# Two loads moved in the SyncE queue of a fused cross-attention kernel: the first keys ahead of the Wv, Wo and row loads, the first batch's values directly behind their write

## The reference

```python
qh = split_heads(q @ Wq.T + bq); kh = split_heads(k @ Wk.T + bk); vh = split_heads(v @ Wv.T + bv)
scores = einsum('bhqd,bhkd->bhqk', qh, kh) / sqrt(32)
scores = where(mask == 0, -1e9, scores)
e = exp(scores - max(scores)) * mask
probs = e / (sum(e) + 1e-09)
attn = einsum('bhqk,bhkd->bhqd', probs, vh)
x = attn @ Wo.T + bo + q
return (x - mean(x)) / sqrt(var(x) + 1e-05) * ln_g + ln_b
```

## Time and profile before

| | us |
|---|---|
| median of 3 runs (lowest, highest) | 617.98 (617.49, 618.96) |
| the profiled execution, its own time | 615.88 |
| span of its trace | 614.1 |
| busy PE / PEld | 564.5 / 456.9 |
| busy DVE / ACT / POOL | 525.6 / 504.6 / 437.5 |

### The profile page before, as it was taken

The page is one execution under the profiler, slowest core; times in us unless marked ns, Lnnn a source line. Parts: engine busy times, 40 slices in busy tenths (PEclk is TensorE's granted clock), DMA queues, the critical chain, the costliest instruction groups (busy, mean ns, idle before and its releaser), DMA issues.

```text
span 614.1 us, 15264 instructions
## 1 busy us (share of the span) xinstructions
PE 564.5 (92%) x5460; PEld 456.9 (74%) x5460; DVE 525.6 (86%) x801; ACT 504.6 (82%) x2288; POOL 437.5 (71%) x399
## 2 busy tenths in 40 slices
PE   2699398999999999999999999999999999999795
PEld 2588376777878788777877788777878788776574
DVE  4577558789998979898998989898998899899877
ACT  4449669899898989998898989998898999889521
POOL 2704443867588795789778886689678967786787
PEclk9989789999999999999999999999999999999899
DMA  8922730120045310640324412340424312202132
GB/s 310 318 88 57 225 88 1 52 99 3 11 140 188 138 53 10 216 147 3 94 93 155 155 64 75 122 148 3 126 76 141 153 51 104 105 2 99 76 138 102
DMA packets 36198, 64.91 MB, mean 106 GB/s; under 512 B 12443, under 2 KB 14491, under 8 KB 34075
## 3 DMA queue, kind: packets, MB, share of 16 engines
q1 hardware_dynamic: 35979, 63.94, 30.6%
q10 hardware_dynamic: 144, 0.00, 0.0%
HBM read 44.15 MB, written 19.46 MB: 104 GB/s over the span
## 4 chain that ended last, share of the span: by engine, by line
PE 84%; DVE 6%; SPq 5%; DMA 3%; issue 2%; POOL 0%; ACT 0%; DVEq 0%
PE qo_bank L420 54%; PE s_bank L420 17%; PE av_bank L508 11%; DVE E L803 2%; DMA Kd<-TP 2%; PE av_bank L420 1%; DMA Vp<-V_scratch 1%; DVE TP L832 1%; SPq L251 1%; SPq L330 1%; SPq L256 1%; DVE qo_bank L849 1%; DVE bn L855 1%; SPq L304 0%; DVE AT_lo L841 0%
## 5 line engine op out<-in xcount | busy, mean ns | idle before, releaser
L625 ACT ACTIVATE E<-E,neg_max 128x77 f32<-128x77 f32 x1024 | 352.2, 352 | 19.7 <-DVE neg_max L811 19.6
L625 ACT ACTIVATION_READ_ACCUMULATOR E<-E,neg_max 128x1 f32 x1024 | 196.8, 192 | 0.0
L1125 POOL TENSOR_TENSOR E<-E,inv_sum 128x1232 f32<-128x1232 f32 x64 | 145.7, 2279 | 66.6 <-DVE inv_sum L818 66.6
L803 DVE TENSOR_TENSOR E<-s_bank,mask_bias 128x616 f32<-128x616 f32 x128 | 101.3, 791 | 40.7 <-PE s_bank L420 38.9
L420 PE MATMUL s_bank<-Kd,QT_hi 128*128 128x308 f32 x512 | 111.7, 305 | 0.0
L832 DVE STREAM_TRANSPOSE TP<-E 128x1280 f32<-128x1280 f32 x64 | 96.1, 1502 | 4.1 <-PE av_bank L508 3.6
L811 DVE TENSOR_REDUCE neg_max<-E 128x8 f32<-128x624 f32 x128 | 98.5, 781 | 0.4
L420 PE MATMUL s_bank<-Kd,QT_lo 128*128 128x308 f32 x256 | 81.3, 317 | 15.5 <-DVE E L803 11.7
L420 PEld LDWEIGHTS s_bank<-Kd,QT_hi 128*128 128x128 f32 x512 | 84.4, 188 | 4.2
L1143 POOL TENSOR_TENSOR Y<-Y,b_row 128x512 f32<-128x512 f32 x62 | 79.2, 1297 | 4.5 <-ACT Y L642 4.2
L1105 POOL TENSOR_TENSOR xT_lo<-xT_raw,xT_hi 128x1024 fp32r<-128x1024 f32 x30 | 71.7, 2410 | 14.0 <-ACT xT_hi L602 14.0
(11 more groups left out here) (60 smaller groups left out, 790.9 us busy)
## 6 DMA issues: line engine op xcount, KB each, us to landing
Y<-in_x SPq DMA_DIRECT2D x16, 1024.0 KB, 6.1
out_y<-Y SPq DMA_DIRECT2D x64, 256.0 KB, 2.0
xT_raw<-in_xT SPq DMA_DIRECT2D x15, 1024.0 KB, 4.9
Vp<-V_scratch SPq DMA_DIRECT2D x32, 96.0 KB, 2.4
K_scratch<-TP SPq DMA_DIRECT2D x1, 1232.0 KB, 6.8
Y<-in_WqT SPq DMA_DIRECT2D x4, 256.0 KB, 8.4
xT_raw<-in_xT SPq DMA_DIRECT2D x2, 512.0 KB, 6.9
TP<-in_WvT SPq DMA_DIRECT2D x4, 256.0 KB, 7.9
```

Of the source, the lines that this page charges most:

```text
L625: last = cp(e, e, ACT.Exp, bias=neg_max[:, t, h:h + 1], accum_out=rowsum[:, t, h:h + 1])
L803: tt(E[:, t, :, 0:SK].rearrange("p (g j) k -> p g j k", g=2), s_bank[:, :, 0:GK].rearrange("p g (j k) -> p g j k", j=HG), mask_bias[:, row ...
L1125: nc.gpsimd.tensor_tensor(out=e, in0=e, in1=inv.unsqueeze(2).broadcast_to((P, 2 * HH, SK)), op=ALU.mult).then_inc(probs_ready, 1)
```

## The change

Nothing is computed differently. load_K(0) moves from stage 0, behind 13 DMA issues, to a place ahead of them, with its wait. load_V(0) and load_V(1) move from behind save_V(1), load_rows(0) and load_rows(1) to directly behind next_xT(2), ahead of these.

```diff
             load_half("k", WkT, 1)
             load_half("q", WqT, 1)
+            load_K(0)
             for c in range(C):
                 load_w("v", WvT, c)
             load_row(bv_loaded, bv_row[:, :], bv)
@@
                 if s == -2:
                     next_xT(0), next_xT(1)
-                elif s == 0:
-                    load_K(0)
                 elif s == 1:
-                    load_K(1), save_K(), save_V(0), next_xT(2)
+                    load_K(1), save_K(), save_V(0), next_xT(2), load_V(0), load_V(1)
                 elif s == 2:
                     save_V(1)
                 elif s == 3:
-                    load_rows(0), load_rows(1), load_V(0), load_V(1)
+                    load_rows(0), load_rows(1)
```

## The result

| | before | changed |
|---|---|---|
| median of 5 runs each, us | 617.98 (617.14 to 618.96) | 611.48 (608.58 to 613.82) |
| the profiled execution / its span | 615.88 / 614.1 | 612.58 / 610.8 |
| busy PE / DVE / ACT / POOL | 564.5 / 525.6 / 504.6 / 437.5 | 566.9 / 525.8 / 504.1 / 438.4 |

The account below looks back on a forecast made before the run. TensorE was taken as the bound nearly throughout, with two long DMA waits, Kd and Vp, in its chain. Gains 3.8 + 1.5 + 0.7 + 1.0 = 7.0 us gave 617.98 - 7.0 = 611.0 us, range 608.3 to 614.2.

Parts of the forecast that it names:

- S(0, 0) earlier: First keys: with Kd landed early, S(0, 0) starts at 26.95 directly behind K(3), 3.8 us won.
- Q(0, 2) at full clock: Behind the removed idle time before S(0, 0), Q(0, 2) takes 2.80 us instead of 4.34, 1.5 us won.
- xT(3), from T0: Values part: xT(3) lands at T0 + 21.9 instead of T0 + 22.6, 0.7 us won, bounds +1.9 and -1.9.
- T0: The moment next_xT(2) is issued, 58.03 us before, forecast at 52.7; values-part times are counted from it.
- from xT(3) to AV(1, 0): ScalarE bounds this stretch after xT(3) lands: 28.7 us instead of 29.65, 1.0 us won, bounds 0 and 1.5.
- AV(1, 0) earlier: Sum of the keys' and values' terms at AV(1, 0): 7.0 us earlier, at 103.3.
- Nothing issued before 7.8 us changes, so that time stands: Premise for load_K(0)'s wait at the start: K_lo(1) still ends at 17.77 us.
- Wv and Wo: Weight loads now issued behind load_K(0): later landing stays hidden, no cost taken; Wv has 1.5 us of cover.
- rival 1: Only the keys pay: xT(3) lands at T0 + 23 to 24.5; 612.1 to 614.5 us, chance 0.24.
- All of TensorE's wait is won: Rival 2, keys 5.3 plus values 9.4 us: about 603, partial form 608; chance 0.12, nearly all partial.
- No fixed time behind 110 us: Behind 110 us only a chain of PE is left, so the shift is carried to the end.
- port rule weighed in the prediction: VectorE two-input and GpSimd instructions lock one SBUF port pair; Wo splits could delay VectorE's Wv split_lo by up to 2.3 us.

Follow-up runs that it names:

- second trace: The changed kernel run once more without further edits, for another trace beside the first: 610.03 us, ratio to before 0.9890.
- late_wv: The changed kernel with the four loads of Wv issued behind the rows of bo, g and b instead of in front of bv: 619.84 us.
- values_only: The kernel before with only load_V(0) and load_V(1) moved, load_K(0) left in its old place: 615.43 us, ratio 0.9965.
- after_xt3: The changed kernel with next_xT(3) moved ahead of save_V(1): 602.66 us, ratio to before 0.9760.

## Why the prediction was right, step by step

| step | forecast | first trace | second trace |
|---|---|---|---|
| S(0, 0) earlier | 3.8 | 2.3 | 3.9 |
| Q(0, 2) at full clock | 1.5 | 1.5 | 1.5 |
| xT(3), from T0 | +0.7 | -0.7 | -0.8 |
| from xT(3) to AV(1, 0) | +1.0 | +1.9 | +2.1 |
| AV(1, 0) earlier | 7.0 | 5.2 | 7.0 |
| span shorter | 7.0 | 3.3 | 5.7 |

(The differences are against the first trace of before. S(0, 0) itself, which no longer follows idle time, is another 0.2 shorter.)

- **Keys.** The mechanism is as forecast, down to the releaser, and the Kd DMAs landed in 2.0 us each. The size is not: S(0, 0) came 2.3 us earlier in the first trace for the 3.8 forecast, since 1.5 were lost before load_K(0) was even issued. K_lo(1) ended at 19.3 and not 17.8, as TensorE began 0.8 us later and K(0), K(1) took 0.7 longer. "Nothing issued before 7.8 us changes, so that time stands" is the premise that did not hold. TensorE's first matmul in before and in the changed kernel, and what ScalarE waited for ahead of it in the latter:

```profile
11.28 0.63 PE L435 MATMUL av_bank<-QT_lo,AT_hi 128*128 128x308 f32 x1 [11.28 <-DVE QT_lo L886]
12.08 0.62 PE L434 MATMUL av_bank<-QT_lo,AT_hi 128*128 128x308 f32 x1 [12.08 <-DVE QT_lo L885]
9.12 0.63 ACT L584 ACTIVATE WqT_hi<-Y 128x512 fp32r<-128x512 f32 x1 [1.11 <-DMA Y<-in_WqT]
```

  This looks like more than a spread from run to run. TensorE began at 10.9 to 11.3 us in the three traces with load_K(0) in its old place, and at 11.4 to 12.2 in the seven with it in front; K_lo(1) began at 16.8 to 17.5 in the three, mean 17.2, and at 17.2 to 18.8 in the seven, mean 18.2. Three traces against seven, without overlap, put 1 us of the keys' gain down to the new order on average: loads whose issue did not change land later (the second 256 KB pieces of Wk 11.4 to 12.1 us after their issue, for 10.8 to 11.1 before). No run shows why. The second trace, with all of the 3.8 us, is the earliest of the seven; S(0, 1) began at 31.4 on average in the six with Wv in its place, for 35.6 in the three: 4.2 us where the forecast had 5.3, and 4.5 (2.7 to 6.2) in the medians. On top of this the start does vary, by 1.6 us among the seven, and before, the wait for Kd up to 30.6 hid that.
- **Clock.** 4.34 to 2.81 us, clock 1.00 over Q(0, 2): right.
- **Wv and Wo.** No cost, right. Wv's low parts were done at 32.7, but bias(0, 1) could not start before S(0, 1) was out, at 33.0. Wo was nearer to its limit than forecast: split by 36.3 and not 31.5. Its issues began at 25.05 and not at about 23, SyncE needed 3.9 us for the four instead of 1.9, and they landed 6.6 to 8.2 us after their issue; VectorE's four split_lo of Wo took 2.90, not 2.49. It stayed hidden: S(0, 1) to T0 is 22.05 us with and without the change. The cover for Wv was smaller than the 1.5 us forecast: GpSimd's last split of it ended at 29.6 and VectorE came to the first at 30.2, and VectorE stood idle for only 0.3 before bias(0, 1). late_wv shows what lies behind it.
- **xT(3).** The other term that was mis-sized, even in its sign: L = T0 + 21.9 was forecast, 23.4 it was, in both traces and in values_only. The issue time was right (T0 + 11.2); the transfer was not. I took 367 GB/s, a rate of one microsecond of the earlier trace rows; from the rows' issue to the landing of xT(3) it was 12.2 us, and less the 1.9 that the forecast had for the start that is 3.15 MB at 306 GB/s (the profile has 301 over 66 to 77 us). 23.4 lies inside the bound given (24.5), and rival 1's condition, xT(3) at T0 + 23 or later, came true.
- **From xT(3) on.** 27.8 and 27.5 us, not 28.7: ScalarE's list from XT_hi(3, 0) to the end of exponent(1, 7) took 22.6 us and not 23.8, since its instructions overlap a little where I added up their durations. This gave back what xT(3) lost, so the part's total was right by luck, by two errors of opposite sign: 1.7 forecast, 1.3 in the traces, 2.2 (1.1 to 3.2) in the medians. The new gap before S(1, 6) came as forecast, though longer (5.6 us for 4), and TensorE was at half clock behind it, 4.70 for Q(2, 2); ScalarE worked on without a break, so nothing of it shows in AV(1, 0).
- **"All of TensorE's wait is won"** was rightly kept small: it needed xT(3) early, and after_xt3 shows 8 us more as soon as it is.
- **"No fixed time behind 110 us"** held to 564 us: from AV(1, 0) to the last scores the shift against the first trace of before changed by 0.4 us at most over 450 us in all nine other traces. The last 50 us are not fixed: 49.3 to 51.0 in ten traces, with TensorE's clock.

What stays open: why the first loads land later with the keys in front, why the first matmuls change their speed at a different time in each run, and why the last stage took 50.4 to 51.0 us in three traces (the changed kernel's two and after_xt3) and 49.3 to 49.5 in the seven others, two of which hold both moves as well; this looks like chance of the clock, but was not settled.

## What to carry to other kernels

When the chain shows an engine waiting for a load, look at which other engine waits at the same time and for what: the first move here freed 8.7 us of TensorE's time and brought about 2, and the same move with the neighbour's load in order brought 17. Order a queue by when each transfer is wanted: 2 MB of rows wanted 40 us later stood ahead of 1 MB that an engine stood idle for. Where a fixed wait goes, the variation it hid comes out, and one trace of each kernel isn't enough to size terms of a microsecond. Nor does a transfer's landing time stand because nothing ahead of it in the queue changed: here about 1 us seems to have gone that way.

## What the runs showed of the hardware

TensorE's first matmuls are slow though the granted clock reads 1.00 there. K(0)'s and K(1)'s of 308 columns took 0.46 us each, and then 0.31, and the change came at any time from 14.7 to 17.6 us in the ten traces; K(0) and K(1) together took 4.9 us in the quickest of the keys-first traces and 6.4 in the slowest. The Trainium skill (TensorE: Matmul & The Clock Gate, "What's actually happening") says that the default state is the throttled one and activity releases it. The durations agree with it, the clock column doesn't show it, so at the start of a kernel the durations decide.

The issue of a DMA isn't of fixed price for SyncE: four of 256 KB took 5.62 us, 2.01 and 3.88. The quick four came when little but the Kd loads was in flight. But before, the four of Wo took 2.06 us too, from 14.43, with the DMA engines fully busy (share 0.99 over 14 to 16 us), so what is in flight isn't the whole of it, and the rule stays open.

Of the port rule weighed in the prediction: in the changed kernel GpSimd's first split of Wo (32.18 to 33.17) met only the last half microsecond of VectorE's split_lo of Wv, and this kept its 2.49 us. In late_wv the two ran side by side, and its timeline has the four at 3.73 us instead of 2.49:

```profile
37.37 3.73 DVE L759 TENSOR_TENSOR AT_lo<-TP,AT_lo 128x512 fp32r<-128x512 f32 x4
38.47 3.66 POOL L1089 CAST WoT_hi<-Y 128x512 fp32r<-128x512 f32 x4
```

That agrees with the Trainium skill (SBUF — State Buffer, "SBUF: two separate sides") in direction: 1.2 us for four, where the forecast had up to 2.3.
